# The query projection of a decoder layer on one core: two plain products of 32-bit numbers, or three products of high and low parts

## The reference, cut to what matters

```
q = (x @ Wq)            # 2048x256 by 256x512, as 8 heads of 64
k, v = context @ Wk, context @ Wv
scores = einsum("bhnd,bhmd->bhnm", q, k) * 64 ** -0.5
out = softmax(scores) @ v   ->  out @ Wo + bo
```

## Time and profile before

| | |
|---|---|
| median of 3 runs | 977.33 us (976.42 to 978.77) |
| profiled execution | 976.84 us, span 975.0 us, mean granted clock 0.976 |
| TensorE busy | 900.7 us (92%) |
| VectorE busy | 550.7 us (56%) |
| ScalarE busy | 343.3 us (35%) |
| GpSimd busy | 554.4 us (57%) |
| attention | from 109.5 us (first transpose) to about 684 us |
| its 16 steps | 35.6 us, then 33.5 to 34.0 us; 40.6 to 41.4 us for p = 0 in the chunks 1 to 3; 40.0 us for the last |

### The profile page before, as it was taken

The page is one execution under the profiler, slowest core; times in us unless marked ns, Lnnn a source line. Parts: engine busy times, 40 slices in busy tenths (PEclk is TensorE's granted clock), DMA queues, the critical chain, the costliest instruction groups (busy, mean ns, idle before and its releaser), DMA issues. The chain is left out here.

```text
span 975.0 us, 13932 instructions
## 1 busy us (share of the span) xinstructions
PE 900.7 (92%) x4616; PEld 537.2 (55%) x4617; DVE 550.7 (56%) x1091; ACT 343.3 (35%) x476; POOL 554.4 (57%) x349
## 2 busy tenths in 40 slices
PE   6988699999999999999999999988899999999990
PEld 2655354455455445465445555544678888756650
DVE  2898556568658557748656746754645121144444
ACT  2245244444425444425443424442441121122212
POOL 0453298888778789759789769872105300022335
PEclk9999899999999999999999999999799999999995
DMA  8013300000001000001000001040794100312115
GB/s 276 17 47 114 98 1 1 22 1 1 1 2 44 23 1 2 1 1 44 22 1 1 1 1 44 1 152 1 193 355 143 43 0 0 118 59 82 51 33 172
DMA packets 43561, 52.86 MB, mean 54 GB/s; under 512 B 3560, under 2 KB 35056, under 8 KB 43504
## 3 DMA queue, kind: packets, MB, share of 16 engines
q1 hardware_dynamic: 37984, 46.30, 14.9%
q0 software_dynamic: 2256, 4.21, 1.2%
q10 hardware_dynamic: 3264, 1.57, 0.6%
HBM read 36.45 MB, written 17.59 MB: 55 GB/s over the span
## 5 line engine op out<-in xcount | busy, mean ns | idle before, releaser
L625 POOL TENSOR_TENSOR accG<-accG,probs 128x1024 f32<-128x1024 f32 (+1 forms) x170 | 404.0, 2377 | 38.1 <-ACT probs L658 20.8
L658 ACT ACTIVATE probs<-st 128x1024 f32<-128x1024 f32 (+1 forms) x208 | 211.4, 1026 | 236.3 <-PE st L854 147.1
L712 DVE TENSOR_REDUCE mxp<-mx 128x1 f32<-128x512 f32 x360 | 231.4, 687 | 91.3 <-PE mx L839 88.4
L883 PE MATMUL av<-probs,V 128*64 128x512 f32 (+1 forms) x832 | 192.4, 600 | 0.0
L839 PE MATMUL mx<-K_hi,Q_hi 64*128 64x512 f32 (+1 forms) x480 | 165.5, 404 | 4.7 <-DVE mxp L712 4.7
L854 PE MATMUL st<-Q_hi,K_lo 64*128 64x512 f32 (+1 forms) x416 | 126.5, 405 | 0.0
L854 PE MATMUL st<-M,ones_r 64*128 64x512 f32 (+1 forms) x416 | 122.7, 398 | 0.0
L854 PE MATMUL st<-Q_hi,K_hi 64*128 64x512 f32 (+1 forms) x416 | 97.8, 442 | 13.0 <-ACT probs L658 13.0
L883 PEld LDWEIGHTS av<-probs,V 128*64 128x64 f32 (+1 forms) x832 | 54.1, 136 | 98.3 <-issue 82.7
L839 PEld LDWEIGHTS mx<-K_hi,Q_hi 64*128 64x128 f32 x480 | 76.2, 184 | 53.2 <-DVE mxp L712 28.9
L854 PE MATMUL st<-Q_lo,K_hi 64*128 64x512 f32 (+1 forms) x416 | 85.7, 391 | 0.0
(11 more groups left out here) (200 smaller groups left out, 1158.9 us busy)
## 6 DMA issues: line engine op xcount, KB each, us to landing
w_gate_up<-in_gate_up SPq DMA_DIRECT2D x4, 2048.0 KB, 19.3
w_down<-in_down SPq DMA_DIRECT2D x2, 2048.0 KB, 15.4
xs<-scratch_sorted_x SPq DMA_DIRECT2D x31, 128.5 KB, 2.0
scratch_sorted_x<-zero SPq DMA_DIRECT2D x7, 514.0 KB, 7.7
xT<-in_xT SPq DMA_DIRECT2D x4, 512.0 KB, 7.9
xring<-in_x SPq DMA_DIRECT2D x4, 512.0 KB, 8.4
scratch_x1b<-xT SPq DMA_DIRECT2D x4, 512.0 KB, 3.0
x<-scratch_x1b SPq DMA_DIRECT2D x4, 512.0 KB, 3.9
```

The costliest lines, as they stand in the source:

```text
L625: pool.tensor_tensor(accG[0:r], so_far[0:r], probs[0:r, (p * KT + t) % RING], ALU.add).then_inc(g_add, 1)
L658: act.activation(probs[0:r, s], st[g % 2][0:r, :], ACT.Exp, scale=DH ** -0.5).then_inc(a_probs, 1)
L712: dve.tensor_reduce(mxp[:, par, h * QT + i, j:j + 1], mx[h][:, 0:kn], AX.X, ALU.max).then_inc(v_mx, 1)
L883: mm = pe.matmul(av[h * DH:(h + 1) * DH, :], V[0:r, t, (2 * p + h) * DH:(2 * p + h + 1) * DH], probs[0:r, g % RING, h * QC:(h + 1) * QC], ...
```

## The change

The projection is given as three products of fp32r parts, W_hi·x_hi + W_hi·x_lo + W_lo·x_hi, six matmuls in place of two. The weights are split into high and low parts once, in the first step; the rows `x1T` are split once for each chunk, for chunk 0 in the first step as well and for the chunks 1 to 3 in the step p = 2 of the chunk before. ScalarE makes the high parts by a copy, VectorE the low parts by a subtraction, each 128x512 at a time (k = 0 and k = 1). The first projection of the attention stage stays as it was. In the diff, the second block of the body is ScalarE's (its calls stand behind `exp(c, p, t)`), then come VectorE's (its calls stand in `after_piece(n)`) and TensorE's.

```
+WEIGHTS_AT, ROWS_AT = (3, 5), (7, 9)
+WEIGHTS_LOW_AT, ROWS_LOW_AT = (7, 10), (14, 19)
...
+        wq_hi, wq_lo = sb("wq_hi", [P, DK, HID], F32R), sb("wq_lo", [P, DK, HID], F32R)
+        x1T_hi, x1T_lo = sb("x1T_hi", [P, DK, QC], F32R), sb("x1T_lo", [P, DK, QC], F32R)
...
+            def weights_high(k):
+                if k == 0:
+                    act.wait_ge(d_wq, 16)
+                act.activation(wq_hi[:, k], wq[:, k], ACT.Copy).then_inc(a_part, 1)
+
+            def rows_high(c, k):
+
+                if k == 0 and not (isinstance(c, int) and c == 0):
+                    act.wait_ge(d_x1Tc, c * 16)
+                act.activation(x1T_hi[:, k], x1T[:, k], ACT.Copy).then_inc(a_part, 1)
...
+                        if first and p == 0 and t in WEIGHTS_AT:
+                            weights_high(WEIGHTS_AT.index(t))
+                        if (first and p == 0 or p == 2 and not last) and t in ROWS_AT:
+                            rows_high(c if p == 0 else c + 1, ROWS_AT.index(t))
...
+            def weights_low(k):
+                dve.wait_ge(a_part, k + 1)
+                dve.tensor_tensor(wq_lo[:, k], wq[:, k], wq_hi[:, k].bitcast(F32), ALU.subtract).then_inc(v_part, 1)
+
+            def rows_low(c, k):
+                dve.wait_ge(a_part, c * DK + (DK + k + 1))
+                dve.tensor_tensor(x1T_lo[:, k], x1T[:, k], x1T_hi[:, k].bitcast(F32), ALU.subtract).then_inc(v_part, 1)
...
+                        if first and p == 0 and n in WEIGHTS_LOW_AT:
+                            weights_low(WEIGHTS_LOW_AT.index(n))
+                        if (first and p == 0 or p == 2 and not last) and n in ROWS_LOW_AT:
+                            rows_low(c if p == 0 else c + 1, ROWS_LOW_AT.index(n))
...
+            def q_proj(pair):
+                terms = [(w, x, k) for w, x in ((wq_hi, x1T_hi), (wq_hi, x1T_lo), (wq_lo, x1T_hi)) for k in range(DK)]
+                for n, (w, x, k) in enumerate(terms):
+                    mm = pe.matmul(mx[0][:], w[:, k, pair * P:(pair + 1) * P], x[:, k, :],
+                                   start=(n == 0), stop=(n == len(terms) - 1))
                 mm.then_inc(p_q, 1)
...
-                        if pair == 0:
-                            pe.wait_ge(d_x1Tc, (c + 1) * 16)
-                        q_proj(pair)
+                        if first and p == 0:
+                            first_q_proj(pair)
+                        else:
+                            if pair == 0 or first and p == 1:
+                                pe.wait_ge(v_part, (c + 1 if pair == 0 else c) * DK + 2 * DK)
+                            q_proj(pair)
```

More of the change, by code:

```diff
@@ L507, in attention @@
         d_wq = sem("d_wq")
+        a_part, v_part = sem("a_part"), sem("v_part")
         d_wo, d_x1Tc, d_x1c, d_x2 = sem("d_wo"), sem("d_x1Tc"), sem("d_x1c"), sem("d_x2")
@@ L820, in _, with first_q_proj @@
             pe.sem_inc(p_mx, STEP_MX - 1)
-            def q_proj(pair):
+            def first_q_proj(pair):
                 for k in range(DK):
@@ L825, in q_proj @@
                                    start=(k == 0), stop=(k == DK - 1))
+                mm.then_inc(p_q, 1)
+            def q_proj(pair):
[3 more added lines that the diff above has]
+                                   start=(n == 0), stop=(n == len(terms) - 1))
                 mm.then_inc(p_q, 1)
```

## The result

| | median | runs | profiled execution | span | mean granted clock |
|---|---|---|---|---|---|
| before | 978.05 us | 4 (976.42 to 979.44) | 976.84 us | 975.0 us | 0.976 |
| after | 1030.26 us | 4 (1029.12 to 1032.51) | 1032.51 us | 1030.7 us | 0.948 |

The ratio is 1.0538, with a 95% interval of 1.0522 to 1.0554: 52 us slower. Forecast were 44 us, range 997 to 1029 us. The sign and the place were right, the size was 8 us short and the time lies 1.3 us outside the range.

A forecast was written before the change was run, and what follows sets the result against it. TensorE was taken as bound by VectorE between the blocks of values and GpSimd at the sums; 25.8 + 12.1 - 1.6 - 2.2 = +34.1 us, plus 9.9 for the clock, gave +44.0, 1021.3 us, range 997 to 1029.

The forecast's parts named there:

- The sign: Whole kernel: slower by over 0.2%, chance 0.92; no change 0.03, faster 0.05.
- the place: Nine splits in VectorE's runs of reductions, in the first step and three steps p = 2, stall TensorE.
- What paces a step: Attention steps: VectorE paces between the blocks of values, GpSimd's adds at the step's end, leaving TensorE next to no slack.
- The projection: 14 projections: 1.56 us in place of 1.88, 0.32 us shorter each; kept in seven steps, 2.2 us, bounds 0 and 4.5.
- the slack: Sums in chunk 0 waited about 0.8 us for GpSimd; in two of four lengthened steps this absorbs 1.6 us.
- The wait for ScalarE: VectorE, mid-run, waits for copies behind exponentials not yet computed; alone 15.9 us in steps p = 2, 8.1 in the first.
- the hold: VectorE's two-SBUF-input subtraction stands until GpSimd's running add ends; stalls with it 25.8 us in steps p = 2, 12.1 in the first.
- Without the hold: Rival at the splits: GpSimd doesn't hold the subtractions; 20.2 us, with up to 9.9 of clock, 997.5 to 1007.4 us; chance 0.2.
- The clock: Behind nine stalls TensorE's clock halves for 3.4 us, 1.1 us lost each: 9.9 us, bounds 0 and 15.3.
- +34.1 us: Whole kernel, all terms but the clock's; also the rival that the clock stays, 1011.4 us, chance 0.2.
- The range: Whole kernel: 997 to 1029 us, from the no-hold rival's low end to the clock's upper bound plus slower copies.

The follow-up runs named there:

- the splits alone: Changed kernel with all splits and waits kept, but the projection again two plain products, the parts made and unused; 1033.95 us, ratio 1.0573.
- high parts alone: Changed kernel with ScalarE's copies early (behind tiles 3 and 4), no low parts made, six products all of high parts; 977.01 us, ratio 0.999.
- the kernel with one input: Changed kernel with VectorE's subtractions replaced by same-size operations with one SBUF input (a copy of the unsplit numbers); 1007.57 us, ratio 1.0288.
- the kernel with TensorE kept at work: Changed kernel with 14 unread matmuls more at each of the nine stalls, also called busy; 1011.96 us, ratio 1.0343.
- placed with the old projection: Changed kernel with splits moved out of VectorE's runs of reductions, one subtraction for two, and the two-product projection of the kernel before; 983.32 us, ratio 1.0044.
- early copies with one input: Changed kernel with ScalarE's copies behind tiles 3 and 4 and low parts by a VectorE operation with one SBUF input; 979.48 us, ratio 1.0011.

## Why the prediction was right or wrong

- **What paces a step** (VectorE between the blocks of values, GpSimd at the sums): right. Each delay of a reduction reached TensorE, and GpSimd's end decided what the shorter projection was worth.
- **The projection and the slack**: the last end came at 1.64 us and not at 1.56, but the steps in which it is kept are 0.3 us shorter, as worked out. In the changed kernel the steps without splits, all but the last of the loop's first turn, are 3.1 us shorter in all, against the 3.8 us (2.2 + 1.6) forecast for saving and slack. The kernel with the splits alone tells the two apart. Beside it these steps are 2.4 us shorter, forecast 2.2: the saving was sized right. The slack was sized too high: its steps p = 1 and p = 3 of chunk 0 are 33.50 and 33.48 us long against 33.81 and 33.72 before, 0.55 us in all and not 1.6. Where no step is delayed, chunk 0 keeps nothing of the saving, and 1.1 us are left.
- **The wait for ScalarE and the hold**: right. Forecast 37.9 us, measured 38.0 with the clock kept up. That the sum fits to 0.1 us is luck: 8.6 forecast against 8.25 measured for each step of p = 2, 12.1 against 13.2 for the first. Of the first step's excess 0.6 us stands also in the kernel with high parts alone, which has no stalls; the rest stays open. Without the hold, 24.0 forecast (15.9 + 8.1) and 23.7 measured.
- **The clock**: the step that failed, as the prediction put it, is "a half-rate stretch of 3.4 us loses at most 1.7 us; a part of it falls into the stall itself or where VectorE paces, so I take 1.1 us: 9 x 1.1 = 9.9 us, with bounds 0 and 15.3". It measured 18.3 us. The mechanism was right; the term was mis-sized, because one row of a short stall, 2.1 us, with one stretch of 3.4 us behind it, was taken for all, and because its cost was taken as 1.1 us where the kernel with one input shows 1.4 to 1.6. Behind stalls of 3.4 to 4.4 us the stretches were mostly 6.8 us, and in the first step, where stalls follow one another, 13.6 us without a break. Half of the 54 us would be 27 us; 18.3 were lost. The upper bound of 15.3 fell with the single stretch, and so did the range.
- The rest, 44 forecast against 52, is this term: 18.3 - 9.9 = 8.4 us. Without it, +34.1 us were forecast, and the kernel with TensorE kept at work is 33.6 us slower than the one before.
- **The range**: its upper end held the clock's loss at 1.7 us for each stall, which was a bound only for the stretch length seen. Rows that showed longer ones were in the same trace, at the stage's start and behind its end, and I didn't use them:

```profile
108.40:115.20 6.80, 3.28 (x5) 1.36 (x5) 0.86 (x2) 0.00 (x0) 0.56 (x4) 0.50 0.74 233
...
681.90:695.40 13.50, 10.54 (x30) 7.28 (x30) 9.76 (x30) 4.84 (x12) 2.67 (x9) 0.50 0.39 112
```

## What to carry to other kernels

An operation is hidden by a neighbour's idle share only if its operands are there when its turn comes. Ask of each wait that is put into a run what releases it and what is queued behind it: here copies of 0.6 us behind the wrong exponentials were worth 20 us with the clock kept up, and moving them gave back 40. A VectorE operation with two SBUF inputs beside a busy GpSimd is priced by GpSimd's instruction and not at its own length (2.3 to 2.8 us here in place of 0.7), and it delays GpSimd too. And when a change makes TensorE stand still again and again, take the upper bound of the clock's cost from the longest half-rate stretches in the trace, and then test it by filling the pauses with matmuls that nobody reads.

## What the runs showed that was not expected

- 126 added matmuls made a kernel 18.3 us faster, since with them the granted clock stayed at 1.00 around the stalls.
- The spread of the runs is 13 us for the splits alone and 10 us for one input (4 runs each), against 3.3 us where the stalls were filled (busy). But unfilled stalls don't always spread: the changed kernel has them, and its 4 runs lie within 3.4 us. In the splits alone the time goes with the mean granted clock: 1027.4, 1032.7, 1035.2 and 1040.5 us at 0.957, 0.954, 0.948 and 0.945. Half-rate stretches that fall differently in each execution may be the cause; that was not tried.
- A half-rate stretch can also fall into a step that has no split, and the last step shows its price. From its transpose to the end of its sums it takes 37.6 to 37.7 us in the three kernels with no such stretch in it (before, placed with the old projection, early copies with one input), 38.8 and 38.9 us in the two with one of 3.4 us, and 39.7 us in the six with one of 6.8 us, the changed kernel and the one with high parts alone among them. So up to 2 us of a profiled time are where such a stretch falls.
- At the end of the loop's first turn TensorE waited for nothing that the profile shows: in the changed kernel the step p = 3 of chunk 1 is 34.70 us long against 33.96, and 35.49 us in the kernel with high parts alone, but 33.87 and 34.02 in others. The cause was not tried and stays open; it is under 1.6 us.
